# Interpolation weights of a channel gate: from a GpSimd chain to ScalarE relus and VectorE products

## The reference, cut to what matters

```
pooled = mean(x, axis=(2, 3))                       # one number per channel
offset = conv1d(pooled, w_offset)                   # 3 taps over the channels
p      = clip(channel + k - 1 + offset, 0, C - 1)   # a fractional channel for each tap k
samp   = (1 - frac) * pooled[floor(p)] + frac * pooled[floor(p) + 1]
out    = sum over k of w_deform[k] * samp[k] + b_deform
x      = gn(x) * sigmoid(out) + x                   # gn: group norm; then the second layer
```

## Time and profile before

| | |
|---|---|
| median of 3 runs | 1546.72 us (1544.78 to 1551.17) |
| profiled execution | 1545.68 us |
| its span, first to last instruction | 1543.9 us |
| PE / PEld busy | 96% / 78% |
| DVE busy | 78% |
| ACT busy | 76% |
| POOL busy | 50% |
| granted TensorE clock, mean | 0.997 |

### The profile page before, as it was taken

How to read it: one execution, slowest core, us unless ns; L and a number is a source line. 1 busy time by engine, 2 the same in 40 slices (tenths; PEclk the granted TensorE clock), 3 DMA queues, 4 the chain that set the end, 5 groups by cost and what they waited for, 6 DMA issues and landing times.

```text
span 1543.9 us, 35552 instructions
## 1 busy us (share of the span) xinstructions
PE 1481.4 (96%) x9287; PEld 1199.6 (78%) x9287; DVE 1211.6 (78%) x4620; ACT 1168.4 (76%) x3044; POOL 776.1 (50%) x2194
## 2 busy tenths in 40 slices
PE   1899999999999999999999999999999999999998
PEld 1587878888887888878888888888887887878776
DVE  6587878888887887878888888888878887878766
ACT  2577777777777777777777777777777777777776
POOL 5544455555465454455454455545455544455520
PEclk9999999999999999999999999999999999999999
DMA  3135453435453445553445553435454445453324
GB/s 132 47 106 160 151 160 114 136 112 162 149 163 107 137 114 154 156 157 113 136 116 155 156 162 113 139 107 162 149 163 119 135 114 154 148 163 113 96 67 138
DMA packets 104276, 205.98 MB, mean 133 GB/s; under 512 B 13584, under 2 KB 83600, under 8 KB 95888
## 3 DMA queue, kind: packets, MB, share of 16 engines
q1 hardware_dynamic: 104080, 203.72, 44.3%
HBM read 51.62 MB, written 51.38 MB: 67 GB/s over the span
## 4 chain that ended last, share of the span: by engine, by line
PE 78%; ACT 7%; DVE 5%; issue 5%; DMA 3%; SPq 1%; POOL 1%; ACTq 0%; DVEq 0%; POOLq 0%
PE ps_s L416 18%; PE ps_o L449 15%; PE ps_p L471 11%; PE ps_v L489 10%; PE ps_p L466 9%; PE ps_t L428 9%; DMA ksp<-kk 3%; PE ps_o L454 3%; ACT eT L599 2%; ACT e L584 2%; DVE e L946 1%; ACT qq L610 1%; ACT hid L634 1%; DVE e L929 1%; SPq L359 1%
## 5 line engine op out<-in xcount | busy, mean ns | idle before, releaser
L584 ACT ACTIVATE e<-e,zmin 128x256 f32<-128x256 f32 x800 | 404.1, 505 | 209.8 <-DVE zmin L929 201.8
L929 DVE CUSTOM_DVE_ANT_0 e<-ps_s,mask 128x256 f32<-128x256 f32 x800 | 337.3, 422 | 150.2 <-PE ps_s L416 144.1
L449 PEld LDWEIGHTS ps_o<-eT,v 128*128 128x128 f32 x2688 | 377.8, 191 | 74.0 <-issue 69.6
L449 PE MATMUL ps_o<-eT,v 128*128 128x128 f32 x2688 | 433.8, 276 | 0.5 <-ACT eT L599 0.3
L416 PE MATMUL ps_s<-kk,qq 128*128 128x256 f32 x1408 | 428.0, 386 | 0.0
L428 PE MATMUL ps_t<-ident,e 128*128 128x128 f32 x1600 | 306.0, 273 | 0.2 <-DVE e L946 0.2
L428 PEld LDWEIGHTS ps_t<-ident,e 128*128 128x128 f32 x1600 | 225.4, 141 | 81.1 <-DVE e L946 0.5
L599 ACT ACTIVATE eT<-ps_t 128x512 f32<-128x512 f32 (+1 forms) x416 | 235.0, 565 | 63.8 <-PE ps_t L428 61.6
L946 DVE SCALAR_TENSOR_TENSOR e<-e,rz,keep 128x256 f32<-128x256 f32 x480 | 251.6, 524 | 0.0
L416 PEld LDWEIGHTS ps_s<-kk,qq 128*128 128x128 f32 x1408 | 221.4, 192 | 35.7 <-issue 29.5
L471 PE MATMUL ps_p<-hid,w2T 128*128 128x448 f32 x448 | 214.6, 561 | 9.7 <-ACT hid L634 9.7
(11 more groups left out here) (147 smaller groups left out, 1917.8 us busy)
## 6 DMA issues: line engine op xcount, KB each, us to landing
raw<-in_x_dram SPq DMA_DIRECT2D x32, 1568.0 KB, 7.2
out_dram<-raw SPq DMA_DIRECT2D x32, 1568.0 KB, 5.4
v<-v SPq DMA_DIRECT2D x192, 224.0 KB, 3.2
kk<-kk SPq DMA_DIRECT2D x192, 112.0 KB, 2.2
ksp<-kk SPq DMA_DIRECT2D x192, 64.0 KB, 2.5
v<-v_last SPq DMA_DIRECT2D x64, 128.0 KB, 2.9
kk<-kk SPq DMA_DIRECT2D x32, 224.0 KB, 2.9
v<-v_last SPq DMA_DIRECT2D x64, 96.0 KB, 2.7
```

Source lines behind the costliest of these rows:

```text
L449: last = nc.tensor.matmul(o[:, UPIX * (u - 1):UPIX * (u + 1)], v[:, s, u, :], eT[:, UPIX * (base + 2 * u - 1):UPIX * (base + 2 * u + 1)], ...
L584: nc.scalar.activation(e[:, i, :], e[:, i, :], ACT.Exp, bias=zmin[:, i:i + 1], scale=-1.0, accum_out=zs[:, i:i + 1]).then_inc(e_done.next( ...
L929: nc.vector.tensor_tensor_reduce(e[:, i, :], ps_s[(TILES * n.parity() + t) % 2][:, 0:KEYS], mask[:].rearrange("p s h a b -> p (s h a b)"), ...
```

## The change

ACT gets a step a5 at `CH` 24, three slots after a4: three relus turn the absolute values into hats, max(0, 1 - |j - p_k|). DVE's d6 no longer multiplies one summed tile: it multiplies each hat by its tap's weight (a number per partition, `wg_s`) and by `pooled_row` and accumulates each product to one column, `TAP` to `TAP + 2`, waits for them, and adds the three with one more small instruction. POOL's step p4 and the tile `hat_sum` are gone. The semaphore counts behind them move: DVE 18 to 21 steps per image, POOL 36 to 28, ACT 4 to 7.

```diff
-CH = dict(..., d4=20, a4=21, p4=21, d6=25,
+CH = dict(..., d4=20, a4=21, p4=21, a5=24, d6=25,
...
-N_DG, N_PG, N_CG, N_AG = 18, 33 + 3, 6, 4
+N_DG, N_PG, N_CG, N_AG = 21, 25 + 3, 6, 7
...
                             if at == CH["a4"]:
                                 act.wait_ge(dg.sem, dg.count(m, 10))
-                                act.wait_ge(pg.sem, pg.count((m + -1), 13))
+                                act.wait_ge(dg.sem, dg.count(m + -1, 13))
...
+                            if at == CH["a5"]:
+                                act.wait_ge(ag.sem, ag.count(m, 3))
+                                for k in range(TAPS):
+                                    nc.scalar.activation(hats[:, k, 1, :], hats[:, k, 0, :], ACT.Relu, bias=ones[:, 0:1],
+                                                         scale=-1.0).then_inc(ag.next(), 1)
                             if at == CH["a6"]:
-                                act.wait_ge(dg.sem, dg.count(m, 11))
+                                act.wait_ge(dg.sem, dg.count(m, 14))
...
-                        if at == CH["p4"]:
-                            gp.wait_ge(ag.sem, ag.count(m, 3))
-                            def tap(k):
-                                far, hat = hats[:, k, 0, :], hats[:, k, 1, :]
-                                return (lambda: gp.tensor_scalar(hat, far, -1.0, 1.0, ALU.mult, ALU.add),
-                                        lambda: gp.tensor_scalar(hat, hat, 0.0, wg_s[:, 9 + k:10 + k], ALU.max, ALU.mult))
-                            steps(7, *tap(0), *tap(1), *tap(2),
-                                  lambda: gp.tensor_tensor(hat_sum[:], hats[:, 0, 1, :], hats[:, 1, 1, :], ALU.add),
-                                  lambda: gp.tensor_tensor(hat_sum[:], hat_sum[:], hats[:, 2, 1, :], ALU.add))
...
                         if at == CH["d6"]:
-                            dve.wait_ge(pg.sem, pg.count(m, 15))
-                            step(11, nc.vector.scalar_tensor_tensor(junk[:], pooled_row[:], 1.0, hat_sum[:],
-                                                                   ALU.mult, ALU.mult, accum_out=col(ZS)))
+                            dve.wait_ge(ag.sem, ag.count(m, 6))
+                            for k in range(TAPS):
+                                nc.vector.scalar_tensor_tensor(cells[:, k, 0:P], hats[:, k, 1, :], wg_s[:, 9 + k:10 + k],
+                                                               pooled_row[:], ALU.mult, ALU.mult,
+                                                               accum_out=col(TAP + k)).then_inc(dg.next(), 1)
+                            dve.wait_ge(dg.sem, dg.count(m, 13))
+                            step(14, nc.vector.scalar_tensor_tensor(col(ZS), col(TAP), col(TAP + 1), col(TAP + 2),
+                                                                    ALU.add, ALU.add))
```

More of the change, by code:

```diff
@@ L312, in chain_at @@
                     yield m, rel
[L315 to L316 removed]
+        D, SQ, VE, R, T0, PL, POS, ZS, EX, GATE, RG, M1, AV, D1, SQ1, VE1, R1, BM, M1G, TAP = (
+            0, 1, 2, 3, 4, 5, 6, 9, 10, 11, 12, 13, 14, 15, 16, 17, 18, 19, 20, 21)
         X_A, X_B, Y_A, Y_B = 24, 28, 32, 36
@@ L461, in hidden @@
                         if g == 0:
-                            pe.wait_ge(dg.sem, dg.count(m, 17))
-                            pe.wait_ge(pg.sem, pg.count(m, 36))
+                            pe.wait_ge(dg.sem, dg.count(m, 20))
+                            pe.wait_ge(pg.sem, pg.count(m, 28))
                         pe.wait_ge(q_done.sem, q_done.count(m, g))
@@ L772, in chain @@
                         if at == CH["p9"]:
-                            gp.wait_ge(dg.sem, dg.count(m, 14))
-                            steps(23,
+                            gp.wait_ge(dg.sem, dg.count(m, 17))
+                            steps(15,
                                   lambda: gp.tensor_tensor(col(BM), col(D1), col(M1), ALU.subtract),
@@ L780, in chain @@
                         if at == CH["p11"]:
-                            gp.wait_ge(dg.sem, dg.count(m, 16))
-                            steps(26, *rsqrt(col(R1), col(VE1), col(T0)),
+                            gp.wait_ge(dg.sem, dg.count(m, 19))
+                            steps(18, *rsqrt(col(R1), col(VE1), col(T0)),
                                   lambda: gp.tensor_tensor(col(Y_A + m.parity()), col(X_A + m.offset % RAWS), col(R1),
@@ L790, in chain @@
                             gp.wait_ge(cg.sem, cg.count(m + -1, 6))
-                            steps(33,
+                            steps(25,
                                   lambda: gp.tensor_scalar(yb_row[:], ones[:], col(Y_B + i), None, ALU.mult),
@@ L1006, in chain @@
                         if at == CH["d6"]:
-                            dve.wait_ge(pg.sem, pg.count(m, 15))
-                            step(11, nc.vector.scalar_tensor_tensor(junk[:], pooled_row[:], 1.0, hat_sum[:],
-                                                                   ALU.mult, ALU.mult, accum_out=col(ZS)))
+                            dve.wait_ge(ag.sem, ag.count(m, 6))
[6 more added lines that the diff above has]
+                                                                    ALU.add, ALU.add))
                         if at == CH["d7"]:
-                            dve.wait_ge(ag.sem, ag.count(m, 4))
-                            step(12, nc.vector.tensor_scalar(col(EX), col(EX), 1.0, None, ALU.add))
-                            step(13, nc.vector.reciprocal(col(GATE), col(EX)))
+                            dve.wait_ge(ag.sem, ag.count(m, 7))
+                            step(15, nc.vector.tensor_scalar(col(EX), col(EX), 1.0, None, ALU.add))
+                            step(16, nc.vector.reciprocal(col(GATE), col(EX)))
                         if at == CH["d9"]:
                             dve.wait_ge(cg.sem, cg.count(m, 4))
-                            step(14, nc.vector.tensor_tensor(col(D1), col(M1), ps_v[:, 2:3], ALU.subtract))
-                            dve.wait_ge(pg.sem, pg.count(m, 23))
-                            step(15, nc.vector.scalar_tensor_tensor(col(SQ1), col(D1), col(D1), col(AV),
+                            step(17, nc.vector.tensor_tensor(col(D1), col(M1), ps_v[:, 2:3], ALU.subtract))
+                            dve.wait_ge(pg.sem, pg.count(m, 15))
+                            step(18, nc.vector.scalar_tensor_tensor(col(SQ1), col(D1), col(D1), col(AV),
                                                                     ALU.mult, ALU.add))
@@ L1021, in chain @@
                             dve.wait_ge(cg.sem, cg.count(m, 5))
-                            step(16, nc.vector.tensor_scalar(col(VE1), ps_v[:, 3:4], EPS, None, ALU.add))
+                            step(19, nc.vector.tensor_scalar(col(VE1), ps_v[:, 3:4], EPS, None, ALU.add))
                         if at == CH["d13"]:
@@ L1025, in chain @@
                             dve.wait_ge(h_done.sem, h_done.count(m + -2, STRIPS))
-                            step(17, nc.vector.tensor_tensor(b1x[:, m.parity():m.parity() + 1], ps_v[:, 0:1],
+                            step(20, nc.vector.tensor_tensor(b1x[:, m.parity():m.parity() + 1], ps_v[:, 0:1],
                                                              bn_t[:, 0:1], ALU.add))
-                            step(18, nc.vector.tensor_tensor(bias[:, m.parity(), :], ps_v[:, P:2 * P], wobv[:],
+                            step(21, nc.vector.tensor_tensor(bias[:, m.parity(), :], ps_v[:, P:2 * P], wobv[:],
                                                              ALU.add))
```

15 lines of the change are left out of this document (7 added, 8 removed).

## The result

The changed kernel takes 1570.41 us (median of 4 runs, 1568.06 to 1571.59) against 1547.33 us for the kernel before, a ratio of 1.0145 with a 95% interval of 1.012 to 1.017. Forecast were 1562 and a range of 1551 to 1571. It is slower, as forecast, by 23 us instead of 15. The profiled execution took 1571.59 us, with a span of 1569.9 against 1543.9.

What follows compares the result with a forecast made beforehand. PE, busy for 96% of the span, was taken as the bound, waiting in slot 2 for the rewritten chain: 0.58 us for 31 images (18.0) less 2.7 in image 0 gives +15.3 us, forecast 1562, range 1551 to 1571.

Steps and rivals of the forecast that it cites:

- d6 sits on PE's path without slack: DVE slot 0 to PE slot 2: time added at d6 comes out one for one at PE's wait for `hid`.
- POOL's part, 0.30 per image: DVE slot 0: without POOL's copies beside it the scaling L946 is shorter and d6 starts 0.30 us earlier.
- the upper bound: d6's cost if its three products wait for POOL copies, left at one collision's 0.30: 1.17 us more per image.
- Relus at no cost: ACT slot 24: three relus take 0.97 us, seen by DVE just when it is free; new wait costed at 0.01.
- d6 at 1.21 for 0.34: DVE slot 0: three products (0.93) and a sum (0.28) before the reciprocal, 0.87 us more per image.
- 0.58 per image, 18.0 us: Reciprocal at 803.46 instead of 802.88, delaying PE in slot 2 by 0.58 us in each of 31 images.
- PE's wait for `hid` grows from 0.2 to about 0.8: Sign expected in the profile after: PE's slot 2 wait grows so, with L471 at this place in every image.
- The eT copy's delay: ACT's copy shifts and delays the context matmuls by a few tenths, but inside the longer wait for `hid`.
- Image 0, 2.7 us earlier: Prologue, nothing runs beside the chain: the gate's exponential starts at 26.61 instead of 29.35, 2.7 us gained once.
- all that follows moves with it: Image 0: everything after the gate's exponential also comes 2.7 us earlier.
- DMA waits as a place that swallows part of it: Part of rival 2 (0.13): DMA waits later in the image, 3% of the chain, would hide some of the delay.
- rival 1: POOL's copies still collide with DVE in slot 0, so the 0.30 is not won: about 1571 us; chance 0.08.

Runs made afterwards that it cites:

- e3: Kernel before with only DVE's new d6 (three weighted products, each of hat_sum, and the sum of three columns), POOL's hats kept: 1587.01 us, ratio 1.024.
- e9: Changed kernel with POOL held at slot 21 until slot 24's first relu is done, so strip and copies run in slots 0 and 1: 1585.26 us, ratio 1.0244.
- e6: Changed kernel with SP's store of the finished image issued two slots later, behind the key copies: 1551.79 us, ratio 1.0022 against the kernel before.
- e5: Kernel before with SP's store of the finished image issued two slots later, behind the key copies: 1538.14 us, ratio 0.9943.
- e1: Kernel before without POOL's hat steps and nothing in their place; d6 multiplies pooled_row by the first absolute values: 1535.38 us, ratio 0.9912.
- e2: Kernel before with three more relus on ACT in slot 24, written to an unread tile: 1549.17 us, ratio 1.0006.
- e4: Changed kernel with the constant 1.0 in place of the per-partition weight in d6's three products: 1558.07 us, ratio 1.0063 against the kernel before.
- e11: Changed kernel unchanged, measured and profiled a second time: 1565.55 us, ratio 1.0118 against the kernel before.
- e10: Kernel before with five one-column memsets on DVE in slot 15 of each image, making DVE's program as long as the changed one's: 1552.11 us, ratio 1.0027.
- e12: Kernel before unchanged, profiled a second time: a single run of 1549.60 us.
- e7: Against the kernel before: POOL weights pooled_row while idle, one relu of 384 makes the hats, d6 is one product of 384: 1538.46 us, ratio 0.9943.
- e8: e7 with SP's store of the finished image two slots later: 1528.38 us, ratio 0.9881 against the kernel before.

## Why the prediction was right, point by point

- *d6 sits on PE's path without slack.* Right for what is added: e3 (1.08 at d6, 1.08 in slot 2) and e9 come out at PE in full, and e6 against e5 shows 16.1 us with slot 9's waits gone. For what is taken away there were only the 0.20 us of PE's wait (e1).
- *POOL's part, 0.30 per image.* Right in the change: L938 takes 0.48 and the next instruction starts 0.40 after it, 0.31 sooner, and e9 takes it away again. Alone it is worth 0.21 (e1). That the new products would pay as well if POOL's copies were there, as the rule of the Trainium skill says (SBUF — State Buffer, the shared port pair), holds for the third one in e3, 0.58 against 0.34. I had kept this 0.30 for the upper bound alone, where it belonged. The rule is wider than what the trace shows: by it a POOL instruction of another kind that reads SBUF and started first would block DVE too, but beside L752, which had run for 0.3 us and ran for 0.4 more, both took their shortest, in 30 images of the kernel before:

```profile
799.11 0.71 POOL L752 TENSOR_SCALAR hats<-hats,wg_s 128x128 f32<-128x128 f32 x1
799.41 0.48 DVE L946 SCALAR_TENSOR_TENSOR e<-e,rz,keep 128x256 f32<-128x256 f32 x1
```

- *Relus at no cost.* Right: 0.97 us, done at 814.96 where DVE was free at 815.02; e2 shows none.
- *d6 at 1.21 for 0.34.* Right: 0.27 apart, 0.93 to the small sum, 1.19 in all. The per-partition weight was predicted at 0.18 per image from L911, and e4 gives 0.18.
- *0.58 per image, 18.0 us.* 0.54 in each of images 1 to 30; the scaling's 0.40 instead of 0.41, the sum's 0.26 instead of 0.28 and d6 starting at once make the difference. For image 1's gate, in the prologue, the forecast was 0.6 and the same number. `hid` did come 0.57 later behind the first scores (58.76 - 53.64 against 59.44 - 54.89), but the slot ends with POOL's p7, which stood behind copies until 59.78 in the kernel before and now starts right behind DVE's L1010, so only 0.1 was left. Together 16.3.
- *PE's wait for `hid` grows from 0.2 to about 0.8.* It grew to 0.30 only. The eT copy's delay, which I had put inside the longer wait for `hid`, reaches PE before it: the context matmuls start 0.32 later in the slot (0.17 of it recorded as a wait), and `hid` adds the other 0.22.
- *Image 0, 2.7 us earlier.* The chain was: the gate's exponential starts at 26.56 (26.61 forecast) instead of 29.35, and PE's first pass of 448 columns at 36.80 instead of 39.57. But "all that follows moves with it" failed: the first scores are only 1.2 us earlier, 1.0 in the second pair of profiles and 4.3 in e6 against e5. This depends on when PE's passes become fast, the last section's first point, which the prediction had not looked at.
- *DMA waits as a place that swallows part of it.* This is the step that failed in sign. I named the 3% of the chain as something that could hide the delay. They were a wait with some 0.1 us of slack, whose size depends on the run, and the changed kernel pays some 3 us more there. With 16.3 + 3 - 1.2 the sum is 18, what e11 measured; the first measurement has 5 more, of the size by which slot 9 and the runs of one kernel differ.
- *How much of it was luck.* The direction and the path were forecast and are shown. That 18.0 - 2.7 lies near the total is in part luck: the path was put 1.7 too high and image 0's gain 1.5 too high, which cancel, and slot 9 was not in the sum. The 1570.41 lies just inside the range of 1551 to 1571, whose upper end was set for rival 1, the collision in slot 0, and that did not happen.

## What to carry to other kernels

Work taken from an idle engine is worth what it does to others: here POOL's hats were worth nothing as work. Their removal was worth 0.21 us per image alone (e1) and 0.54 to 0.60 beside the long d6 (e3 and e9 against the changed kernel), because DVE's instructions take longer beside the copies that had stood behind the hats. A saving on a path counts only as far as the wait at its end goes; a cost counts in full. Before moving work to a busier engine, find the one stretch in which a later engine waits for it, and count there every start-to-start distance, the wait for one's own results among them. When a saving and a cost meet on one path, fewer and wider instructions (one product of 384 for three of 128 and a sum) can keep the saving and lose the cost.

## What the runs showed of the hardware

- In the prologue PE's passes of 448 columns take twice as long up to some moment, and the moment is not fixed. Two passes take 1.7 to 1.9 us before it and 0.9 to 1.0 after it. The kernel before, the changed one, and e5, whose prologue is that of the kernel before:

```profile
42.14 1.86 PE L471 MATMUL ps_p<-hid,w2T 128*128 128x448 f32 x2 [0.51 <-ACT hid L634]
...
47.32 0.92 PE L466 MATMUL ps_p<-raw,w1x 128*128 128x448 f32 x2
```

```profile
45.21 1.70 PE L465 MATMUL ps_p<-raw,w1x 128*128 128x448 f32 x2
```

```profile
48.02 1.70 PE L466 MATMUL ps_p<-raw,w1x 128*128 128x448 f32 x2
```

  In e6, with the changed kernel's prologue, the passes at 44.53 are fast already (0.92). So kernels with the prologue of before start their first scores between 54.7 and 56.4 us (before, e5, e10, e12), and those with the changed one between 52.1 and 53.7 (changed, e6, e11). The granted clock of the slow stretch is recorded as 1.00, the level of 2.4 GHz, but these passes last as long as those at a recorded 0.50, the level of 1.2 GHz. That level comes a second time in the kernel before, from 59.43 to 66.26 us, after PE had been idle for 1.96 us. Below are the pass and the stretch; the stretch's row has its length, busy us and count of PE, PEld, DVE, ACT and POOL, and then granted clock, DMA share and GB/s:

```profile
59.44 1.86 PE L471 MATMUL ps_p<-hid,w2T 128*128 128x448 f32 x2 [1.96 <-ACT hid L634]
```

```profile
59.50:66.20 6.70, 6.59 (x15) 3.87 (x16) 3.82 (x15) 3.80 (x10) 4.70 (x17) 0.50 0.16 45
```

  The changed kernel has such a stretch too (58.1 to 64.9), but the second profile of before, e1, e7, e8 and e9 have none. In slots 2 to 4 of image 0 it costs 2.4 us (10.15 in the kernel before, 7.78 in its second profile). What decides it is not shown.
- A per-partition scalar makes the three-operand product of 128 elements 60 ns longer than a constant does (347 against 287 ns, e4).
- Where a small copy has some 0.1 us of slack behind a large store, PE waits for it by 9 to 21 us over the run, and nearly all of it in images in which an instruction fetch (2.3 MB of DMA over the span) falls near it. Once the store is issued behind the copies, 0.2 to 0.4 us are left (e5, e6, e8).
